# Two steps of the later groups' first product, moved on TensorE: where the low-rank second products stand

## The reference, cut to what matters

```python
# block 1
u  = conv(x) + cond @ c_weight.T + bias          # grouped convolution, 9 taps
y  = u @ W.T + b + (u @ A[ad].T) @ B[ad].T        # A, B: rank 16, one of 3 adapters or none, by sample
x1 = x + y
# block 2
v      = (softmax(mlp(cond)) mixes 8 kernels, 64 x 64) @ x1 + bias   # per sample
scores = v @ Wr.T; gates = softmax(top 16 of 64)
out    = x1 + ((v @ A2.T) * gates) @ B2.T * 2
```

## Time and profile before

| | us |
|---|---|
| median of 3 runs | 657.33 |
| the profiled execution | 656.7 |
| its span, first to last instruction | 654.9 |
| PE busy (share of the span) | 648.1 (99%) |
| DVE busy | 451.4 (69%) |
| ACT busy | 214.0 (33%) |
| POOL busy | 73.8 (11%) |

### The profile page before, as it was taken

One profiled execution on the slowest core, in us unless ns is written; L12 is line 12 of the kernel. 1 busy time (PEld: TensorE's weight loads), 2 busy tenths in 40 slices (PEclk: granted clock), 3 DMA queues, 4 the chain that ended last, 5 costly groups with the idle time before them and its releaser, 6 DMA issues.

```text
span 654.9 us, 8354 instructions
## 1 busy us (share of the span) xinstructions
PE 648.1 (99%) x3197; PEld 537.7 (82%) x3197; DVE 451.4 (69%) x690; ACT 214.0 (33%) x275; POOL 73.8 (11%) x91
## 2 busy tenths in 40 slices
PE   9999999999999999999999999999999999999997
PEld 8878888888897788888889788888879888888885
DVE  2859469549377788558769758636967856665785
ACT  2714135233144024335115312333423421433420
POOL 1598200000000160000000042000000000000000
PEclk9999999999999999999999999999999999999999
DMA  8587714986969926776976682287797664037795
GB/s 303 210 293 279 299 50 144 356 246 218 392 228 379 356 100 260 280 223 245 366 275 220 261 318 97 102 225 245 290 325 264 273 248 184 0 118 203 211 345 221
DMA packets 51594, 157.98 MB, mean 241 GB/s; under 512 B 5488, under 2 KB 6384, under 8 KB 51568
## 3 DMA queue, kind: packets, MB, share of 16 engines
q1 hardware_dynamic: 46240, 148.05, 62.7%
q10 hardware_dynamic: 5328, 9.61, 4.8%
HBM read 131.94 MB, written 25.71 MB: 241 GB/s over the span
## 4 chain that ended last, share of the span: by engine, by line
PE 91%; DVE 3%; DMA 3%; issue 1%; SPq 1%; ACT 0%; DVEq 0%
PE bank L1374 25%; PE bank L1376 24%; PE bank L1375 24%; PE bank L1388 9%; PE bank L1408 3%; DMA piece_lo<-kept 2%; PE bank L1395 2%; PE bank L1414 1%; PE bank L1402 1%; PE bank L1400 1%; PE bank L1415 1%; DVE x L925 1%; DMA gate<-hidden_w 1%; DVE u_lo L1012 1%; DVE work L932 1%
## 5 line engine op out<-in xcount | busy, mean ns | idle before, releaser
L893 DVE TENSOR_TENSOR piece_lo<-raw,piece_hi 128x1024 fp32r<-128x1024 f32 x60 | 74.1, 1239 | 90.0 <-ACT piece_hi L647 89.8
L647 ACT ACTIVATE piece_hi<-raw 128x1024 fp32r<-128x1024 f32 x60 | 63.4, 1058 | 147.1 <-PE bank L1376 103.2
L1374 PE MATMUL bank<-piece_hi,u_hi 128*128 128x512 f32 x272 | 107.9, 397 | 0.0
L1376 PE MATMUL bank<-piece_hi,u_lo 128*128 128x512 f32 x272 | 107.3, 395 | 0.0
L1375 PE MATMUL bank<-piece_lo,u_hi 128*128 128x512 f32 x272 | 107.3, 394 | 0.0
L1374 PE MATMUL bank<-v_hi,piece_hi 128*128 128x512 f32 x256 | 101.8, 398 | 0.0
L1376 PE MATMUL bank<-v_hi,piece_lo 128*128 128x512 f32 x256 | 101.1, 395 | 0.0
L1375 PE MATMUL bank<-v_lo,piece_hi 128*128 128x512 f32 x256 | 101.0, 394 | 0.0
L1374 PE MATMUL bank<-piece_hi,v_hi 128*128 128x512 f32 x192 | 76.0, 396 | 0.8 <-DMA piece_lo<-kept 0.8
L1376 PE MATMUL bank<-piece_hi,v_lo 128*128 128x512 f32 x192 | 75.8, 395 | 0.0
L1375 PE MATMUL bank<-piece_lo,v_hi 128*128 128x512 f32 x192 | 75.8, 395 | 0.0
(11 more groups left out here) (143 smaller groups left out, 800.7 us busy)
## 6 DMA issues: line engine op xcount, KB each, us to landing
raw<-pieces SPq DMA_DIRECT2D x76, 512.0 KB, 5.5
piece_hi<-kept SPq DMA_DIRECT2D x48, 512.0 KB, 4.7
piece_lo<-kept SPq DMA_DIRECT2D x48, 512.0 KB, 5.8
x<-x SPq DMA_DIRECT2D x16, 512.0 KB, 5.3
gate_x<-gates ACTq DMA_DIRECT2D x32, 256.0 KB
out<-x SPq DMA_DIRECT2D x32, 256.0 KB, 4.8
conv_in<-conv_x SPq DMA_DIRECT2D x15, 516.0 KB, 7.1
conv_in<-pieces SPq DMA_DIRECT2D x12, 512.0 KB, 8.8
```

Source lines behind the costliest of these rows:

```text
L647: act.activation(piece_hi[:, n % SLOTS, :], raw[:, r % RAWS, :], ACT.Copy).then_inc(s_piece_hi, 1)
L893: dve.tensor_tensor(piece_lo[:, n % SLOTS, :], raw[:, r % RAWS, :], piece_hi[:, n % SLOTS, :].bitcast(F32), ALU.subtract).then_inc(s_piece ...
L1374: pe.matmul(to, left_hi, right_hi, start=first, stop=False)
L1376: return pe.matmul(to, left_lo, right_hi, start=False, stop=last)
```

## The change

Only PE's order changes. The second quarter's four instructions follow the first quarter's at once, ahead of product 5. The third quarter's four go between the two pieces of product 6, which is cut into `winograd_piece(12, 0)` and `winograd_piece(12, 1)`. No other engine's code is changed, and no instruction is added or taken away.

```diff
+                def winograd_piece(n, j, to, hi, lo, rows, stop):
+                    if n + j in RAW:
+                        raw_ready(n + j)
+                    else:
+                        fetched(n + j)
+                    for s in range(2):
+                        for c in range(2):
+                            k = 2 * j + c
+                            mm = product(banks[to[s]][:, :], rows(hi, k, s), rows(lo, k, s),
+                                         *columns_piece(n + j, c), k == 0, stop and k == 3)
+                        if j or s:
+                            mm.then_inc(s_win, 1)
+
                 def winograd(n, to, hi, lo, rows, stop):
                     for j in range(2):
...
+                        winograd_piece(n, j, to, hi, lo, rows, stop)
...
                 for s in range(2):
                     lora_second(1, s, 1 - s, False)
+                for s in range(2):
+                    lora_second(0, s, 6 + s, False)
                 sum_ready(4)
                 pe.wait_ge(s_f, g * 24 + 6)
                 winograd(10, (2, 3), v_hi, v_lo, sum_of(S3), True)
-                for s in range(2):
-                    lora_second(0, s, 6 + s, False)
+                pe.wait_ge(s_f, g * 24 + 12)
+                winograd_piece(12, 0, (1, 0), u_hi, u_lo, block_of(1, 1), False)
                 pe.wait_ge(s_f, g * 24 + 8)
                 for s in range(2):
                     lora_second(1, 2 + s, 4 + s, True)
-                pe.wait_ge(s_f, g * 24 + 12)
-                winograd(12, (1, 0), u_hi, u_lo, block_of(1, 1), False)
+                winograd_piece(12, 1, (1, 0), u_hi, u_lo, block_of(1, 1), False)
                 for s in range(2):
                     lora_second(0, 2 + s, 1 - s, False)
```

## The result

| | before | after |
|---|---|---|
| median of 22 runs each | 656.65 us | 658.04 us |
| ratio, 95% interval | | 1.002 (1.0013 to 1.0026) |
| the profiled execution, its span | 656.7, 654.9 | 658.33, 656.5 |

The change makes the kernel slower by 1.39 us (658.04 − 656.65), 0.2%; the interval is 0.9 to 1.7 us. The first three runs of the kernel before, from which the prediction started, lay at 657.33; over 22 it is 656.65. Single runs scatter far more than the three did: 655.65 to 657.71 before, 656.34 to 659.48 after. That matters for all that follows; where in the kernel it comes from, as far as the profiles show, is at the end.

A forecast was written before the change was run, and what follows sets the result against it. PE, busy 99% of the span, was taken as the bound, in a ring with ACT and DVE; delays of 0.33, 0.93 and 0 us in groups 1 to 3 sum to 1.26, giving 658.6 us from 657.33, range 657.6 to 659.3.

The forecast's parts named there:

- PE issues the same list; only growing waits matter: On PE: no instruction added or removed; a new order could save by itself only 0.5 us of waits for DVE's rests.
- Product 5 is 0.93 late: On PE: four instructions of 0.2325 us ahead of product 5 delay it, ACT's splits 14 and 15 and DVE's split 14.
- The second quarter's early banks: Banks 6 and 7 are ready earlier, worth nothing, since DVE reads them after six adds that wait for product 5.
- the third quarter's place: Between product 6's pieces: its products end at 236.8 us, DVE wants banks 4 and 5 not before 238.3; covered by 1.5.
- The meeting with POOL: DVE's run beside POOL's additions: blocking changes the 0.93 us delay to 0.33 in group 1 and 0.93 in group 2.
- a common slowing: Alternative reading of DVE and POOL: both just run slower; groups 1 and 2 lose about 0.56 us each, 1.1 in all.
- the edge of what can be told: Whole run: 0.2% is 1.31 us, and the forecast lies on that line; 0.28 of its 0.50 chance above, 0.22 below.
- The other order in group 2: Rival: DVE's split 14 starts ahead of POOL's multiplication, decided by 0.10 us; loss 0.66 us, 658.0 us; chance 0.17.
- The whole shift: Rival: the adds meet POOL worse than counted and the full 0.93 passes twice, 1.86 us, 659.2 us; chance 0.15.
- Unseen slack in group 2: Rival: PE's own pace, not the rest, held group 2's score; only group 1's 0.33 us remains, 657.7 us; chance 0.10.
- The four adds in group 1: Rival, not slower: DVE's four adds meet one POOL instruction less, returning over 0.93 us; 656.8 us at best; chance 0.08.
- the two gates: Group 2's first `mix` and first score: part of the 0.93 us shows at the first, the rest by the second.

The follow-up runs named there:

- POOL moved away: POOL's additions of groups 1 and 2 start only when the gates are transposed, in the kernel before and the changed one: ratios 0.9991 and 0.9983 against the kernel before.
- the two single moves: Against the kernel before, only the second quarter's products moved, or only the third quarter's: ratios 1.0014 and 1.0000.
- the half move: The change with only one of the second quarter's two products ahead of product 5, against the kernel before: ratio 1.0001, stages +0.46 us.
- the late split 15: DVE's split 15 behind the fifth chunk, in group 1 behind the last rest, in the kernel before and the changed one: ratios 0.9991 and 0.9999 against the kernel before.
- four kernels here: Kernel before and changed kernel, split 15 and combined weights' rests later in two variants, changed ones with POOL's additions later: ratios 0.9995, 0.9995, 1.0002, 1.0004 against the kernel before.
- before, split 15 fifth: Kernel before with split 15 behind the fifth chunk's addition in all groups, group 1's combined weights' rests later, SP's queue unchanged: ratio 1.0002 against the kernel before.

## Why the prediction was right

- *PE issues the same list; only growing waits matter.* Shown: groups where no wait grows (group 3, and all groups with POOL moved away) are equal to 0.02 us.
- *Product 5 is 0.93 late, and splits 14 with it.* Measured 5.96 against 5.02 us into the stage, 0.94.
- *The second quarter's early banks are worth nothing; the third quarter's place costs nothing.* Shown by the two single moves, +1.28 and −0.04.
- *The meeting with POOL, counted instruction by instruction.* Forecast 0.33, 0.93 and 0 in the three groups; measured 0.34, 0.92 and 0.01. Split 14 forecast at 1.33 and 1.6, measured 1.34 and 1.60; split 15 at 1.22, measured 1.21. It was the blocking that decided and not a common slowing, which would have cost both groups 0.56; and the half move costs 0.35 and 0.11. The written-out steps give 0.69 − 0.37 = 0.32 and 1.29 − 0.37 = 0.92, each 0.01 less than the figure behind them.
- *Sum 1.26, 658.6 us.* The stages give 1.27, the medians 1.39. The profile's span grew by 1.6 us, of which 0.63 came ahead of the change and 0.27 was lost after group 2's mixing in the kernel before only, at 480 us; 1.27 + 0.63 − 0.27 is 1.63. The time came out 0.56 lower than 658.6 because the starting point was 0.68 lower, and the change 0.13 more than forecast. The interval of the whole runs, 0.9 to 1.7 us, would also hold the 1.1 of a common slowing; that 1.39 lies so near to 1.26 is in part luck, and only the stage times tell the accounts apart.
- *That the change stands at the edge of what can be told.* So it was: 1.39 us against 1.31, at 22 runs an interval of 0.13 to 0.26% slower. It is slower, and on which side of 0.2% is not settled.
- *The rivals.* The other order in group 2 would have shown split 14 at 1.22, and it took 1.60. The whole shift would have cost group 1 0.93, and it cost 0.34. Unseen slack in group 2 is refuted by the new bracket of 0.32 at its score. The four adds in group 1 returned 0.12 us and not a whole POOL instruction, so the run did not get faster.
- Missed: the 0.5 us of PE's list was taken for all that there was to win. The stage times say three times that: groups 1 and 2 were 1.28 and 0.24 longer than group 3, and kernels with another order on DVE got 1.51 of it.
- Missed: PE's waits for DVE rose to 0.9 in the list and not to 1.8. The list does not hold the late first `mix`, nor the second `mix` instruction, which starts 0.10 us late; only the distances between starts have it all. And the two gates were called one delay, which is true of its price and not of its remedy, as the late split 15 showed.
- Two readings were wrong without harm. The POOL addition that took 1.81 us ended at 388.49 + 1.81 = 390.30, 0.59 after the split's end at 389.71, and not 0.13; a full 0.74 from 0.15 before that end fits it. And 60 PE instructions, not 24 + 16, lie between the first quarter and the mixing stage, the same 60 in both orders.

## What to carry to other kernels

When an instruction list is only reordered on an engine that is busy all the time, look for the ring: the product that is put later, who waits for it, and whether that comes back to the engine; an early result helps only if its reader's own order lets it be read early. Two engines that block each other make the price of a delay a matter of tenths of a us of phase, so count it out from the rows, or better move one of them to where nobody waits for the other. A stage made faster is a gain only if what comes behind it keeps up: four kernels here gained 1.5 us in the stage and nothing that the whole runs show.

## What the runs showed of the hardware

- DVE and POOL instructions that both read two SBUF operands go one after the other, whole: a POOL multiplication of 0.62 us took 1.49 behind a split, a split of 1.22 us took 1.81 behind a POOL addition. DVE's adds with one operand in a bank kept their 0.60 us from start to start throughout. With durations and starts of one profile the meetings at a new phase came out within 0.02 us, which I had not expected of an effect that turns on 0.10 us.
- PE's clock fell behind a wait. In the profile with 2.45 us of idle PE ahead of 305.20 us, the granted clock was 0.56 in the 3.4 us that follow, and instructions started 0.43 us apart instead of 0.23. Behind the wait of 1.41 us in the profile of the kernel "before, split 15 fifth" it stayed at 1.00 (304.2 to 307.6 us).
- In the fourteen profiles the unsteady part of this kernel is ahead of the change. The first low-rank product of group 1 lay between 224.78 and 226.97 us in kernels that are alike up to there, behind waits at 7 us (for the convolution's taps, 0.22 us in the kernel before and up to 1.35 in others), at 182 to 191 us (for DVE, whose splits there wait over ACT for raw pieces) and at 213 to 216 us (for fetched pieces). From there to the last score of a group, kernels with the same order differ by 0.03 us at most. Whole runs of one kernel scatter by 2 to over 5 us, and one stage can still be read to hundredths. Where the slowest of those runs lose their time no profile shows.
